# A dynamic-programming alignment whose two direction flags are computed in four large VectorE operations between the passes instead of in every forward step

## The reference

```python
def _dtw_cost(D):
    row0 = jnp.cumsum(D[0])
    def row_step(prev_row, d_row):
        first = d_row[0] + prev_row[0]
        def col_step(left, inp):
            d_ij, up, diag = inp
            r = d_ij + jnp.minimum(jnp.minimum(up, left), diag)
            return (r, r)
        ...
def _backtrack(R, T1, T2):
    def step(carry, _):
        ...
        choice = jnp.argmin(jnp.stack([cd, cu, cl]))   # diagonal, up, left
        ni = jnp.where(choice <= 1, i - 1, i)
        nj = jnp.where((choice == 0) | (choice == 2), j - 1, j)
        ...
x = x + _L0_xattn_ref(ctx_1024, _layernorm(x, axis=-1))
x = x + _L0_ffn_ref(_layernorm(x, axis=-1), ...)
```

## Time and profile before

| | us |
|---|---|
| median of three runs | 453.04 |
| lowest and highest | 452.05 and 455.96 |
| span of the profiled execution | 482.3 |

### The profile page before, as it was taken

How to read it: one execution, slowest core, us unless ns; L and a number is a source line. 1 busy time by engine, 2 the same in 40 slices (tenths; PEclk the granted TensorE clock), 3 DMA queues, 4 the chain that set the end, 5 groups by cost and what they waited for, 6 DMA issues and landing times.

```text
span 482.3 us, 10815 instructions
## 1 busy us (share of the span) xinstructions
PE 341.2 (71%) x2360; PEld 261.1 (54%) x2361; DVE 357.9 (74%) x2007; ACT 214.8 (45%) x588; POOL 154.5 (32%) x182
## 2 busy tenths in 40 slices
PE   5860100007995197798699996999989998898982
PEld 4750100007995064445354554987877887786541
DVE  4958999999999918878567933566666666666687
ACT  3655100002215826858464112555555565553691
POOL 8000100000000000466566762255555545455200
PEclk9995555555555598899799998899999999999998
DMA  8503898990001010122222566445544544453994
GB/s 326 204 5 87 259 296 209 195 315 27 27 1 54 17 34 1 46 88 88 89 78 94 197 225 206 123 130 156 147 132 139 146 113 120 129 137 122 416 387 166
DMA packets 48360, 69.10 MB, mean 143 GB/s; under 512 B 10486, under 2 KB 38588, under 8 KB 46655
## 3 DMA queue, kind: packets, MB, share of 16 engines
q1 hardware_dynamic: 41327, 51.61, 35.4%
q0 software_dynamic: 6864, 16.86, 9.9%
q10 hardware_dynamic: 128, 0.16, 0.1%
HBM read 39.33 MB, written 31.24 MB: 146 GB/s over the span
## 4 chain that ended last, share of the span: by engine, by line
PE 39%; DVE 14%; issue 11%; SPq 10%; ACT 8%; POOL 6%; DMA 5%; DVEq 4%; another core or an unknown queue 2%; POOLq 0%; ACTq 0%
PE psT L1145 7%; POOL slot_rows L617 6%; PE psT L1135 6%; PE psD L945 5%; PE psC L1135 4%; PE psT L938 3%; ACT psC L717 3%; SPq L429 3%; DMA xk<-in_x 2%; PE psD L1125 2%; SPq L434 2%; ACT back L837 2%; PE psT L1033 2%; SPq L452 2%
## 5 line engine op out<-in xcount | busy, mean ns | idle before, releaser
L617 POOL DMA_INDIRECT slot_rows<-stage,slot x64 | 62.7, 979 | 51.5 <-DVE slot L1467 19.8
L1033 PE MATMUL psT<-x2T,sw 128*128 128x512 f32 x128 | 59.4, 608 | 0.0
L938 PE MATMUL psT<-ident,xk 128*128 128x128 f32 x64 | 15.3, 425 | 60.7 <-DMA xk<-in_x 60.7
L1145 PE MATMUL psT<-w,hgT 128*128 x158 | 50.7, 402 | 10.3 <-DVE ys_far L1553 4.6
L626 POOL DMA_INDIRECT results<-ys_near,idx x40 | 39.5, 988 | 48.5 <-PE psC L1135 22.2
L626 POOL DMA_INDIRECT results<-ys_far,idx x39 | 38.4, 985 | 30.7 <-issue 14.3
L938 PEld LDWEIGHTS psT<-ident,xk 128*128 128x128 f32 x64 | 13.8, 242 | 60.7 <-issue 60.7
L709 ACT ACTIVATE xT<-psT 128x512 f32<-128x512 f32 x16 | 8.7, 594 | 84.7 <-PE psT L938 84.7
L1135 PE MATMUL psT<-xsT,w_now 128*128 128x128 f32 x320 | 44.6, 284 | 1.7 <-DVE w_now L1560 1.6
L819 ACT ACTIVATE xsT<-psD 128x256 f32<-128x256 f32 x79 | 29.4, 372 | 36.5 <-PE psD L1125 32.1
L1560 DVE COPY w_now<-w 128x256 f32 x79 | 25.8, 327 | 23.7 <-issue 15.7
(11 more groups left out here) (247 smaller groups left out, 824.2 us busy)
## 6 DMA issues: line engine op xcount, KB each, us to landing
xs<-slot_rows SPq DMA_DIRECT2D x79, 129.0 KB
back<-results SPq DMA_DIRECT2D x8, 1024.0 KB, 12.8
slot_rows<-fill SPq DMA_DIRECT2D x32, 129.0 KB, 5.3
xc<-in_x SPq DMA_DIRECT2D x4, 1024.0 KB, 8.8
xk<-in_x SPq DMA_DIRECT2D x4, 1024.0 KB, 12.2
out<-xk SPq DMA_DIRECT2D x7, 512.0 KB, 6.5
w<-in_L_ffn_We SPq DMA_DIRECT2D x1, 2048.0 KB, 13.2
b<-in_L_ffn_be SPq DMA_DIRECT2D x1, 2048.0 KB
```

The source lines that it names most:

```text
L617: pool.indirect_dma_start(out=slot_rows, out_offset=bass.IndirectOffsetOnAxis(ap=slot[:, w, T:T + 1], axis=0), in_=stage[:, T, :], in_offs ...
L938: mm = pe.transpose(psT[n % 2][c][:, k, :], xk[:, 4 * n + k, c * P:(c + 1) * P], ident[:, :])
L1033: mm = pe.matmul(psT[m][w][:, :, :].rearrange("p a b -> p (a b)"), (sw1, sw3)[w][:, c, m * P:(m + 1) * P], x2T[:, g, c, :], start=(c == 0) ...
L1145: pe.matmul(psY[c % 2], hgT[:, (c - 2) % 4, :], w2f[:, bass.ds(e, D)], start=True, stop=True).then_inc(y_done, 1)
```

## The change

The flag of line 1300 and the call of `left_wins` leave the forward step. After the last step four operations compute the same two flags, each over half of the 108 steps (54 rows of 32 columns, 1728 columns), the upper half first. The second flag still overwrites the minimum in M. There is no wait between the four and none behind them before the memset.

```diff
-            def left_wins(t):
-
-                dve.tensor_tensor(M[:, t, 1:W], R[:, t + 1, 0:CH], M[:, t, 1:W], ALU.is_lt)
-
             right = [QUAD - 1] + list(range(QUAD - 1))
             for t in range(NT):
 ...
                 start(dve.tensor_tensor(M[:, t, 1:W], R[:, t, 0:CH], R[:, t, 1:W], ALU.min))
-
-                dve.tensor_tensor(F[:, t, 1:W], R[:, t, 0:CH], R[:, t, 1:W], ALU.is_le)
                 settle()
                 start(dve.tensor_tensor_scan(R[:, t + 1, :], M[:, t, :], cst[:, t, :], BIG,
                                              ALU.min, ALU.add))
-                if t:
-                    left_wins(t - 1)
                 settle()
 ...
-            left_wins(NT - 1)
+            HT = NT // 2
+            for rows, after in ((slice(HT, NT), slice(HT + 1, NT + 1)), (slice(0, HT), slice(1, HT + 1))):
+                dve.tensor_tensor(F[:, rows, 1:W], R[:, rows, 0:CH], R[:, rows, 1:W], ALU.is_le)
+                dve.tensor_tensor(M[:, rows, 1:W], R[:, after, 0:CH], M[:, rows, 1:W], ALU.is_lt)
             link(dve.memset(cst[:, :, CH:W], 1.0))
```

## The result

The changed kernel took 459.71 us (458.79 to 460.97, four runs), the kernel before 453.38 us (452.05 to 455.96, four runs). The ratio is 1.0142, with a 95% interval of 1.0099 to 1.0186: slower by 6.3 us, between 4.5 and 8.4. The forecast was 461.2 us in a range of 457.8 to 464.4.

The account below looks back on a forecast made before the run. DVE, with no slack and tied with PE's path at the mask's turn, was taken to bound the kernel. Terms 0 + 0 + 7.4 + 0.8 = +8.2 us on 453.04 us gave 461.2 us, range 457.8 to 464.4.

Parts of the forecast that it names:

- a tie: Before the mask's turn: the mask's path from DVE and PE's unused matmuls end within 0.05 us of each other.
- The flags cost nothing in the step: Forward step: both flags lie under waits, so removing them gains 0; bounds 3.2 us gain for both, step stays 0.55 us.
- The comparison of linked operations in the routing and of step 0: Evidence without a flag between: routing starts 0.21 to 0.23 us apart, step 0 scan to shuffle 0.27 us, as with flags.
- The large operations: Between last scan and memset: four operations of 1.96 us, 7.62 us together, net +7.4 us after the last small flag.
- The clock at the unused matmuls: Before the mask's turn: PE idles some 7 us, matmuls then run partly at low clock; 0 to +1.9 us, taken +0.8.
- the DVE terms: DVE's passes: 0 for the first flag, 0 for the second, +7.4 us net for the four large operations.
- the 29.3 us between span and median: Whole kernel: unprofiled median lies 29.3 us below the 482.3 us span; the difference of +8.2 us was carried over unchanged.
- rival A: Before the unused matmuls: a later path over PE and ACT hides some or all of 7.4 us; 453 us, chance 0.06.
- The rule of the skill: DVE: minimize operations, since the pipe empties after each; 215 fewer and 4 more would gain, while rows say 7.4 us loss.
- B (slots): Forward step: flags cost 0.12 and 0.13 us slots, net 19.5 us faster, 433.5 us; chance 0.03 of over 1% faster.
- C (more than the sum): Behind 177 us, clock shifts, or large operations slower than their slope: 464 us and above, chance 0.10.

Follow-up runs that it names:

- the pairs above: Changed kernel against kernel before, measured in three sets with 16 unused matmuls, ratios 1.0142, 1.0134 and 1.0199, and once with 10 in both, 457.58 against 451.49 us.
- the second profile of before: Kernel before run again with no edit, 483.98 us against 483.5 us, ratio 1.0014; its profile has unused matmuls of 6.57 us.
- the first pair: First profiles of the changed kernel and the kernel before, DVE's passes 127.57 against 120.55 us; measured times 459.71 against 453.38 us.
- the three profiles of the changed kernel: Changed kernel unedited, profiled at its first measurement and two repeats: 459.71, 489.98 and 460.35 us.
- the first set: Runs compared with the kernel before at 483.5 us; the unedited changed kernel took 489.98 us there, ratio 1.0134.
- the third: Set with the kernel before at 451.79 us; changed kernel 460.35 us; with 10 instead of 16 unused matmuls, before 451.49 us, changed 457.58 us.
- the three measurements: Changed kernel, unedited, against the kernel before three times: 459.71 against 453.38 us, 489.98 against 483.5 us, 460.35 against 451.79 us.

## Why the prediction was right, point by point

**What bounds the kernel.** DVE had no slack, and what DVE was late all that follows was late: shown by the pairs above, where 7.0 to 7.3 us on DVE come out as 6.3 to 8.6 us. The picture of a tie was too strong. It stands in the profile that I had, but in the second profile of before DVE was later by 3.85 us. That DVE has no slack holds in both.

**The flags cost nothing in the step.** Right. The steps kept 0.55 us. From the first minimum to the last scan, the pass took 108.53 - 48.74 = 59.79 us before and 108.35 - 48.81 = 59.54 us after (59.67 us in the second profile). The gain is 0.1 to 0.25 us, against bounds of 3.2 us for both flags. The comparison of linked operations in the routing and of step 0 was the step on which all rested, and the runs bear it out.

**The large operations.** 1.96 us and three times 1.95 us against 1.96 us forecast, and 7.62 us for all four against 7.62 us. DVE's passes grew by 127.57 - 120.55 = 7.0 us in the first pair, where +7.4 us was forecast. The rest is the 0.25 us of the pass and 0.10 us between the memset and the last mask row (169.29 - 109.04 = 60.25 us before, 176.38 - 116.23 = 60.15 us after).

**The clock at the unused matmuls.** I took +0.8 us, and this is the term on which the runs don't agree. The matmuls did run longer after the idle time (6.03, 6.49 and 6.24 us in the three profiles of the changed kernel, 4.36 us in the first of before), as said. Against that first profile the term is larger than forecast: the turn stood 4.71 us behind the start of the last mask row, and in the changed kernel it stood 5.99, 6.45 (183.08 - 176.63) and 6.20 us behind it, 1.3 to 1.7 us more. Against the second profile of before, with 6.52 us, it is nothing or slightly less than nothing. I had named this case (PE's path ending well before DVE's, nothing added), and it came in one of two profiles. The medians go both ways too: 6.5 us for the change in the first set, less than DVE's 7.3 us, and in the third 8.6 us with 16 matmuls and 6.1 us with 10.

So 0.8 us is a mean of cases and not a size that any pair showed. In the result the difference is 6.3 us instead of 8.2 us, 1.9 us less: 0.4 us are DVE's. The other 1.5 us may be this term or something behind the turn; that wasn't shown, and the three measurements of the same change differ by 2.3 us among themselves. That the time lies well inside the range is owed to the DVE terms, which were right, and in part to the width of the range.

**The profiled execution.** I took the 29.3 us between span and median for the drawing out by the profile. That was wrong: the runs of that set took as long without one. The argument against rival A, that profiling draws out DMAs and queues, rests on the same reading, and no run supports it; A was ended by PE's idle time. The error did no harm to the sum, since the passes are DVE's own durations and were the same on all chips.

**The rule of the skill.** The Trainium skill, "VectorE: DVE Perf Modes", section "Rules for kernel authors", asks for fewer operations. The run with 216 small operations in a row agrees: 0.103 us for each, and 14.6 us less with four large ones. The changed kernel has 212 operations fewer than the kernel before (216 small ones out, 4 large ones in) and is slower, so in this kernel the rule holds only for operations that nothing covers.

**Rivals.** A (hidden) fell with PE's idle time before the mask. B (slots) fell with the added operations, which cost the same with the flags in the steps. C (more than the sum) asked for 464 us and above, 11 us more than before. The largest of the three measurements is +8.6 us, near the forecast's own 8.2 us, and the large operations ran at their slope, so nothing speaks for it.

## What to carry to other kernels

Where DVE waits for its own last result, the wait is room for one independent operation of the size measured here (32 columns), and moving that operation out frees time that nobody can use. Before batching small operations, look at the distance between the starts of the two instructions around each of them, and find a place in the same trace where nothing stands between: if the distances are equal, the operation is free, and its batched form is not if it stands where nothing covers it. Fewer instructions and less busy time are no gain in themselves: DVE was busy for 1.1 us less after the change (357.9 and 356.8 us on the pages) and the kernel 6.3 us slower.

## What the hardware showed that I had not expected

- A wait of DVE for its own operation of 32 columns hides one other such operation: the second costs 0.08 us under the wait for the minimum and 0.06 to 0.07 us under the wait for the scan, near the 0.103 us that it costs with no wait at all.
- The same kernel before takes 483.5 us in one set and 452.4 and 451.8 us in two others, each on a chip of its own, with DVE's passes equal within 0.03 us in the two profiles of it at 482 us and, in the changed kernel, within 0.25 us between spans of 458.0 and 493.2 us. What differs lies behind the mask. From 215 to 265 us, in windows of 10 us, the DMAs moved 101 to 107 GB/s in the changed kernel's profile with 458.0 us and 85 to 94 GB/s in that with 493.2 us. Whether that is the cause or follows from it, and whether it goes with the chip or with the time of the set, isn't shown.
- The 16 unused matmuls took 4.36 us in one profile of the kernel before and 6.57 us in the other. In the first profile of the changed kernel they start at 176.72 us. The granted clock is 0.50, which is 1.2 GHz, in the windows up to 181 us, and 0.68 in the window from 181 to 182 us, so they ran at 1.2 GHz for almost five of their six microseconds. The windows show PE, PEld, DVE, ACT, POOL busy, clock, DMA share, GB/s:

```profile
177.00:178.00 1.00, 1.00 (x4) 0.34 (x3) 0.00 (x0) 0.00 (x0) 0.00 (x0) 0.50 0.31 98
...
180.00:181.00 1.00, 1.00 (x4) 0.35 (x3) 0.00 (x0) 0.00 (x0) 0.00 (x0) 0.50 0.30 106
181.00:182.00 1.00, 1.00 (x5) 0.39 (x4) 0.00 (x0) 0.00 (x0) 0.00 (x0) 0.68 0.00 0
```
